# Softmax sums by ones in the values, two of eight copies of distances moved to ScalarE, and probabilities turned two steps after they are made

## The reference

```python
h = _layernorm(x) * (1 + ca) + sa
Q, K, V = h @ Wq + bq, h @ Wk + bk, h @ Wv + bv          # 16 heads of 8
scores = Q @ K.T / sqrt(8) + einsum('bhid,ijd->bhij', Q, rel_table[clip(j - i + 64, 0, 128)])
ctx = softmax(scores) @ V
x = x + ga * (ctx @ Wo + bo)
h = _layernorm(x) * (1 + cb) + sb
x = x + gb * ffn(h)      # a router picks 2 of 8 experts for each token
```

## Time and profile before

| | |
|---|---|
| median of 3 runs | 684.85 us (684.81 to 685.73) |
| profiled execution: time, span | 685.29, 683.6 us |
| busy: PE, PEld | 588.5 us (86%), 439.8 (64%) |
| busy: DVE, ACT, POOL | 507.1 (74%), 508.8 (74%), 423.3 (62%) |
| copies of distances, DVE L1267 | 125 of 0.945 us in the page |
| exps, ACT L711 | 512 of 0.504, and 512 reads of the accumulator of 0.196 |
| turns, PE L968 | 1024 transposes |

### The profile page before, as it was taken

One profiled execution on the slowest core, in us unless ns is written; L12 is line 12 of the kernel. 1 busy time (PEld: TensorE's weight loads), 2 busy tenths in 40 slices (PEclk: granted clock), 3 DMA queues, 4 the chain that ended last, 5 costly groups with the idle time before them and its releaser, 6 DMA issues. The chain is left out here.

```text
span 683.6 us, 17706 instructions
## 1 busy us (share of the span) xinstructions
PE 588.5 (86%) x5108; PEld 439.8 (64%) x5108; DVE 507.1 (74%) x1888; ACT 508.8 (74%) x1578; POOL 423.3 (62%) x543
## 2 busy tenths in 40 slices
PE   5667789999899899899989989978798989999950
PEld 4444556666666566566666656655577979999940
DVE  6788988999999999999999999997565312222127
ACT  4157799999999999999989999998643434444434
POOL 2660655747668687686776966855366765554535
PEclk9777999999999999999999999999999999999975
DMA  5996678778787788778868878874525777565538
GB/s 142 308 230 202 198 235 248 228 235 248 214 245 241 213 252 246 228 219 260 249 208 242 252 213 247 243 236 148 189 82 174 236 234 228 198 217 185 176 97 274
DMA packets 173125, 149.03 MB, mean 218 GB/s; under 512 B 16182, under 2 KB 162642, under 8 KB 173030
## 3 DMA queue, kind: packets, MB, share of 16 engines
q1 hardware_dynamic: 168054, 139.33, 67.9%
q0 software_dynamic: 4544, 8.44, 3.7%
q10 hardware_dynamic: 432, 0.14, 0.1%
HBM read 83.71 MB, written 65.05 MB: 218 GB/s over the span
## 5 line engine op out<-in xcount | busy, mean ns | idle before, releaser
L711 ACT ACTIVATE P<-NS,nmax 128x256 f32<-128x256 f32 x512 | 254.2, 504 | 50.5 <-DVE nmax L1312 49.6
L1312 DVE CUSTOM_DVE_ANT_0 NS<-psS,bias 128x256 f32<-128x256 f32 x512 | 185.2, 417 | 2.3 <-PE psS L950 1.6
L968 PE MATMUL psT<-ident,P 128*128 128x128 f32 x1024 | 140.0, 281 | 8.9 <-ACT PT L722 8.8
L1267 DVE COPY stage<-psDist 128x768 f32<-128x768 f32 x125 | 118.1, 945 | 33.9 <-issue 25.2
L722 ACT ACTIVATE PT<-psT 128x512 f32<-128x512 f32 x256 | 136.4, 586 | 0.0
L968 PEld LDWEIGHTS psT<-ident,P 128*128 128x128 f32 x1024 | 118.2, 145 | 24.0 <-issue 9.8
L778 ACT ACTIVATE F<-psS,b1T 128x256 f32<-128x256 f32 x156 | 65.4, 471 | 86.5 <-PE psS L1061 86.5
L609 POOL DMA_INDIRECT results_d<-y,row_u x78 | 76.0, 974 | 56.7 <-DVE y L1458 40.8
L711 ACT ACTIVATION_READ_ACCUMULATOR P<-NS,nmax 128x1 f32 x512 | 100.3, 196 | 0.0
L950 PE MATMUL psS<-Kst,Qst 32*128 32x256 f32 x512 | 65.9, 336 | 34.7 <-DVE nmax L1312 29.9
L1061 PE MATMUL psS<-xT,w 128*128 128x256 f32 x312 | 80.6, 381 | 0.3 <-DMA w<-in_L_ffn_w_dram 0.3
(11 more groups left out here) (254 smaller groups left out, 1044.2 us busy)
## 6 DMA issues: line engine op xcount, KB each, us to landing
dist_d<-stage SPq DMA_DIRECT2D x128, 384.0 KB, 3.0
bias<-dist_d SPq DMA_DIRECT2D x256, 192.0 KB, 3.3
w<-in_L_ffn_w_dram SPq DMA_DIRECT2D x39, 512.0 KB, 3.7
x<-slots_d SPq DMA_DIRECT2D x39, 129.0 KB, 3.0
y<-results_d SPq DMA_DIRECT2D x16, 256.0 KB, 5.0
dist_d<-zeros SPq DMA_DIRECT2D x1, 2048.0 KB, 14.4
out_dram<-y SPq DMA_DIRECT2D x8, 256.0 KB, 3.2
results_d<-y,row_u POOLq DMA_INDIRECT x78, 3.0
```

The lines of the kernel that those rows point to most:

```text
L711: act.activation(P[:, p % 2, h, q, :], NS[:, p % 2, h, q, :], ACT.Exp, scale=-1.0, bias=nmax[:, p % 2, k:k + 1], accum_out=lsum[:, b % 2, ...
L968: mm = pe.transpose(psT[:, h, S * k + 128 * q:S * k + 128 * q + 128], P[:, p % 2, h, q, 128 * k:128 * k + 128], ident[:])
L1267: dve.tensor_copy(stage[:, p % STAGES, :, :, :], bank[:, :, 0:2 * RW].rearrange("p h (q c) -> p h q c", q=2)).then_inc(dist_out, 1)
L1312: dve.tensor_tensor_reduce(NS[:, p % 2, h, q, :], psS[:, h, S * q:S * q + S], bias[:, p, h, q, :], 1.0, 3e38, ALU.add, ALU.min, nmax[:, p ...
```

## The change

1. *Sums by ones.* The values `V` get a column of ones beside each head's eight columns (16 to a head), two groups of heads share 32 columns, and `psO` is used whole: the row sums come out of `weigh`. The exps lose `accum_out`. `inverses`, `widen`, `spread_l` and `sums` go. ACT copies `psO` to `C` (`copy_values`, p3), PE transposes it, four transposes (`turn_values`, p3), and DVE takes reciprocals and multiplies in `context`, now in p4 behind the minima. The context has tokens on partitions then: PE transposes it (`ct`, p4, in place of `y`), ACT copies it to `ctxT`.
2. *Gains.* `ga` is folded into the weights: for each batch the extra `gain` (p7) spreads two rows over the partitions by matmuls, and DVE makes `boR` and `WoG`. POOL adds the bias to `X` (`add_bias`). The extra `y` (p6) projects with `WoG`; DVE adds it to `X`.
3. *Copies.* In p0 and p4 (`BY_ACT_OUT`) of batches above 0, ACT does the copy of distances, behind its exps and gathers.
4. *Turns.* Probabilities are turned two steps behind (`BEHIND`), with three buffers `P`; `W_SLOTS` follows. ACT's exps stand ahead of the takes.
5. *Loads.* `Wo` and `bv` are permuted on the host: two transfers for eight.

```diff
+BY_ACT_OUT = (0, 4)
 M_SLOTS = ((("q23", 1),), (("k01", 1),), (("k23", 1),), (("logits", -3), ("v", 1)),
-           (("y", -1), ("nh", 2)), (("u01", -2),), (("u23", -2),), (("q01", 2),))
-X_SLOTS = ((), (("rank", -4),), (("turn", -2),), (("back", -2),), (("tally", 1 - B),), (("rows", -3),), (("t", -1),), ())
+           (("ct", -1), ("nh", 2)), (("u01", -2),), (("u23", -2),), (("q01", 2),))
+X_SLOTS = ((), (("rank", -4),), (("turn", -2),), (("back", -2),), (("gains", 0), ("tally", 1 - B)), (("rows", -3),),
+           (("y", -1),), (("gain", 0),))
-W_SLOTS = ((2, (1,)), (3, (0,)), (3, (1,)), None, (0, (0, 1)), (1, (0,)), (1, (1,)), (2, (0,)))
+W_SLOTS = ((2, (0,)), (2, (1,)), (3, (0, 1)), None, (0, (0,)), (0, (1,)), (1, (0,)), (1, (1,)))
+BEHIND = 2
-BY_ACT = ("y", "nh", "back")
+BY_ACT = ("ct", "nh", "back")
...
# SP
-            for a in range(4):
-                at = slice(32 * a, 32 * a + 32)
-                sp.dma_start(WoD[at, :], Wo.rearrange("(g a d) e -> a g d e", a=4, d=D)[a]).then_inc(weights_in, 16)
-                sp.dma_start(bvT[at, :], bv.rearrange("(g a d x) -> a g d x", a=4, d=D, x=1)[a],
-                             allow_slow_non_contiguous=True).then_inc(weights_in, 16)
+            sp.dma_start(WoD[:], Wo).then_inc(weights_in, 16)
+            sp.dma_start(bvT[:], bv.rearrange("(e a) -> e a", a=1)).then_inc(weights_in, 16)
...
# POOL
+            def add_bias(r):
+                at = slice(2 * r, 2 * r + 2)
+                pool.wait_ge(x_dve, X_TAKEN["gain", r][0])
+                pool.tensor_tensor(X[:, at, :], X[:, at, :], rep(boR[:], 1, 2), ALU.add).then_inc(biased, 1)
...
# ACT
-                past(act, turned, 2 * (s - 1))
+                past(act, turned, 2 * (s - BEHIND))
...
-                    act.activation(P[:, p % 2, h, q, :], NS[:, p % 2, h, q, :], ACT.Exp, scale=-1.0,
-                                   bias=nmax[:, p % 2, k:k + 1],
-                                   accum_out=lsum[:, b % 2, q, a, p // 2:p // 2 + 1]).then_inc(exp_done, 1)
+                    act.activation(P[:, s % (BEHIND + 1), h, q, :], NS[:, p % 2, h, q, :], ACT.Exp, scale=-1.0,
+                                   bias=nmax[:, p % 2, k:k + 1]).then_inc(exp_done, 1)
...
+            def copy_values(b):
+                act.wait_ge(values_done, HG * b + HG)
+                past(act, ctx_full, b)
+                act.activation(C[:], psO[:], ACT.Copy).then_inc(c_copied, 1)
+
+            def put_out(n):
+                act.wait_ge(dist_done, n + 1)
+                act.wait_ge(written[(n - STAGES) % SLOTS], 16 * ((n - STAGES) // SLOTS) + 16)
+                act.activation(stage[:, n % STAGES, :, :, :],
+                               psD[:, :, 0:2 * RW].rearrange("p h (q c) -> p h q c", q=2), ACT.Copy)\
+                    .then_inc(dist_out, 1)
...
                 if p == 3 and b > 0:
-                    sums(b - 1)
+                    copy_values(b - 1)
+                exps(b, p)
                 for name, of in M_OF.get(at, ()):
                     if name in BY_ACT:
                         act.wait_ge(m_full, M_DONE[at][0] + 1)
                         take(name, of, psM)
-                exps(b, p)
-                if (b, p) > (0, 0):
-                    gather(*at)
+                if PAIRS * b + p >= BEHIND:
+                    gather(*shifted(b, p, -BEHIND))
+                if act_puts_out(b, p):
+                    past(act, x_dve, so_far(X_DONE, b, p)[1])
+                    past(act, x_act, so_far(X_DONE, b, p)[2])
+                    put_out(PAIRS * b + p + AHEAD)
...
# PE
+                elif name == "gain":
+                    for k in range(2):
+                        mm = pe.matmul(spare[:, k, :], ident[:, r:r + 1].broadcast_to([128, 128]), gR[:, k, :],
+                                       start=True, stop=True)
...
+            def turn_values(b):
+                pe.wait_ge(c_copied, b + 1)
                 for q in range(2):
-                    mm = pe.transpose(psO[:, S + 128 * q:S + 128 * q + 128],
-                                      linvD[:, q, :, :, :].rearrange("p a g d -> p (a g d)"), ident[:])
+                    for r in range(2):
+                        mm = pe.transpose(psO[:, S * q + 128 * r:S * q + 128 * r + 128],
+                                          C[:, S * r + 128 * q:S * r + 128 * q + 128], ident[:])
                 mm.then_inc(ctx_full, 1)
...
# DVE
+                elif name == "gain":
+                    dve.tensor_copy(boR[:], spare[:, 1, :])
+                    i = dve.tensor_tensor(WoG[:], WoD[:], spare[:, 0, :], ALU.mult)
...
             def context(b):
-                dve.wait_ge(lrow_done, b + 1)
+                values = psO[:].rearrange("p (n m d) -> p n m d", n=4, d=2 * D)
+                dve.wait_ge(ctx_full, b + 1)
+                dve.reciprocal(linv[:], values[:, :, :, D:D + 1].rearrange("p n m d -> p n (m d)")).then_inc(linv_done, 1)
                 if b > 0:
-                    dve.wait_ge(m_full, M_FULL["y", b - 1])
-                dve.tensor_tensor(ctxT[:], psO[:, 0:S], lrow[:], ALU.mult).then_inc(ctx_done, 1)
+                    dve.wait_ge(m_full, M_FULL["ct", b - 1])
+                dve.wait_ge(linv_done, b + 1)
+                dve.tensor_tensor(ctx_r[:].rearrange("p q (r m d) -> p (q r) m d", r=2, d=D), values[:, :, :, 0:D],
+                                  rep(linv[:], 3, D), ALU.mult).then_inc(ctx_done, 1)
...
+                if p == 4 and b > 0:
+                    context(b - 1)
...
-                if p == 0 and b > 0:
-                    inverses(b - 1)
...
-                if p == 3 and b > 0:
-                    context(b - 1)
...
-                if n < STEPS:
+                if n < STEPS and not act_puts_out(b, p):
```

More of the change, by code:

```diff
@@ L645, in _ @@
                     stack(b + 1, (b + 1) % 2, 2)
+                if b > 0:
+                    add_bias(b - 1)
                 for r in SENDS.get(b, ()):
@@ L656, in _ @@
                     mix(b - 2, 0)
+            add_bias(B - 1)
             normalise_again(B - 2)
-            widen(B - 1)
             mix(B - 3, 1)
@@ L729, in take @@
                 else:
[L730 to L731 removed]
+                    i = act.activation(ctxT[:], bank[:, 0:S], ACT.Copy)
                 i.then_inc(m_act, 1)
@@ L797, in _ @@
             for b in range(B):
-                if b == 1:
-                    act.wait_ge(taken, 3)
                 for p in range(PAIRS):
                     step(b, p)
-            gather(B - 1, PAIRS - 1)
+            for p in range(PAIRS - BEHIND, PAIRS):
+                gather(B - 1, p)
             act.activation(p1[:, 0:1], ident[:, 0:1], ACT.Silu)
-            sums(B - 1)
-            act.wait_ge(m_full, M_FULL["y", B - 1])
-            take("y", B - 1, banks[1])
+            copy_values(B - 1)
+            act.wait_ge(m_full, M_FULL["ct", B - 1])
+            take("ct", B - 1, banks[1])
             units(0, 1)
@@ L862, in project @@
                                        hT[:, 128 * k:128 * k + 128], Wv_s[:], start=True, stop=True)
-                elif name == "y":
+                elif name == "ct":
                     pe.wait_ge(ctx_done, b + 1)
-                    mm = pe.matmul(bank[:, 0:S], WoD[:], ctxT[:], start=True, stop=True)
+                    for k in range(2):
+                        mm = pe.transpose(bank[:, 128 * k:128 * k + 128], ctx_r[:, k, :], ident[:])
                 elif name in ("u01", "u23"):
@@ L898, in extra @@
                         mm = pe.transpose(spare[:, k, :], h2T[:, 128 * k:128 * k + 128], ident[:])
-                elif name == "t":
-                    pe.wait_ge(m_act, M_TAKEN["y", r][1])
+                elif name == "y":
+                    pe.wait_ge(m_act, M_TAKEN["ct", r][1])
+                    pe.wait_ge(x_dve, X_TAKEN["gain", r][0])
                     for k in range(2):
-                        mm = pe.transpose(spare[:, k, :], yT[:, 128 * k:128 * k + 128], ident[:])
+                        mm = pe.matmul(spare[:, k, :], ctxT[:, 128 * k:128 * k + 128], WoG[:], start=True, stop=True)
+                elif name == "gains":
+                    pe.wait_ge(taken, 3)
+                    pe.transpose(spare[0:B, 0, :], modT[:, 2, :], ident[:])
+                    mm = pe.transpose(spare[0:B, 1, :], gabo[:], ident[:])
+                elif name == "gain":
+                    for k in range(2):
+                        mm = pe.matmul(spare[:, k, :], ident[:, r:r + 1].broadcast_to([128, 128]), gR[:, k, :],
+                                       start=True, stop=True)
                 elif name == "tally":
@@ L1023, in step @@
                     extras()
-                if (b, p) > (0, 0):
-                    turn(*before(b, p))
+                if PAIRS * b + p >= BEHIND:
+                    turn(*shifted(b, p, -BEHIND))
                 if p in X_LATE:
@@ L1033, in step @@
                     weigh(b - int(p < 4), g, halves)
-                    if p == 2:
```

(11 more changed lines are left out.)

80 lines of the change are left out of this document (34 added, 46 removed).

## The result

The changed kernel takes 699.97 us (median of 4; 698.87 to 704.78) beside 685.02 for the kernel before on the same chip: a ratio of 1.0226, 95% interval 1.0194 to 1.0258, slower by about 15. The profiled execution took 699.71, its span is 698.0; before it was 683.6.

A forecast was written before the change was run, and what follows sets the result against it. It took PE and DVE as almost equal in p0 to p5, with PE's work filling the time to p5's scores, and DVE binding from p5. Terms summed to +6.35, giving a 691.2 us median; 8 in 10 range 668 to 697.

The forecast's parts named there:

- Even batches ...: to p5 0, then unchanged, `gain` 0.4: Even batches 4 to 14: nothing lost up to p5, later steps unchanged, `gain` 0.4 each; 6 x 0.4 = 2.4 slower.
- a lighter ACT: All steps: ACT lighter by about 1.6 a batch, booked at nothing because PE and DVE set the steps.
- Odd batches: Odd batches 5 to 13: `gain` 0.4 plus 0.45 for `rank` less 0.1, 5 x 0.75 = 3.75 slower.
- the term for `rank`: p1 of odd batches from 5: PE, and DVE with it, waits 0.45 for ACT's copy ahead of `rank`.
- gain: End of p7: DVE's pair of instructions adds 0.4 a batch with nothing to cover it; ends 0.25 and 0.7.
- Prices: Instruction costs: ACT's copy 0.79 (0.59 to 0.96), exps 0.40 apart, 29 copies on ACT, DVE's p0 step 2.08.
- Turning two steps behind: PE's wait for gathers, 0.3 a batch, goes; 0.1 taken in batches other than even ones; ends 0 and 0.3.
- Batches 1 to 3: First batches after batch 0: 0.3 slower each, 3 x 0.3 = 0.9.
- Start: Before the first minimum: six fewer early issues on SP let distance writes land sooner, 1.3 off; ends 0 and 2.1.
- Last batch and closing: Last batch and end: ACT's saved reads against an added turn, gathers, chain and `add_bias`; 0, ends -2 and +2.
- The faster one: DVE's copies stop waiting for PE; p5's scores under 17.0 after the batch's first minimum; 666 us (655 to 683), chance 0.30.
- No change: ACT's copies come before PE does, and savings in p0 and gathers pay for `gain`; 685 us within 0.2%, chance 0.12.

The follow-up runs named there:

- e8: Changed kernel with two links of the choice moved: `chosen` from p6 to p7, `ahead_of` from p5 to p6; 693.88 us, 1.0109 of the kernel before.
- e13: Changed kernel with both links moved, and ACT's copy of p0 ahead of its gathers in odd batches from 5 on; 690.76 us, 1.0077 of the kernel before.
- e10: Changed kernel with both links moved, DVE's two `gain` instructions cut to a one-column copy in every batch but the first; 686.77 us, 1.0001 of the kernel before.
- e16: Changed kernel with both links moved and probabilities turned one step behind in place of two; 690.57 us, 1.0083 of the kernel before.
- e6: Kernel before, with only the exps' sums into the accumulator left out (a constant 16 instead); 688.30 us, 1.0019 of the kernel before.
- e12: Kernel before with both links moved and `Wo` and `bv` loaded whole in place of eight pieces; 681.61 us, 0.9941 of the kernel before.
- e3: Changed kernel with ACT's copy of distances ahead of the two gathers of its step; 700.10 us, 1.0223 of the kernel before.
- e7: Changed kernel with both links moved, `gain` in next batch's p0, ACT's p0 copy before its gathers, no ACT copy in the last batch; 691.06 us, 1.0080.

## Why the prediction was wrong

**The step that failed** is "Even batches ...: to p5 0, then unchanged, `gain` 0.4", and with it the booking of a lighter ACT at nothing because "PE and DVE set the steps". Up to p5 it held: the scores of p5 begin 17.9 to 18.2 after the batch's first minimum in the even batches, 17.99 in the mean (17.8 forecast). Then p6 was not unchanged. The sum counted what a faster ACT would spare and not what it would set off: the tanh, hence POOL's product, 0.37 earlier, into an instruction of DVE that cleared it by 0.11 before. That is 0.88 in each of six batches, 5.3 of the 8.0 that the sum is short. With both links moved the kernel takes 693.88 (e8), near the forecast 691.2; part of that is luck, since the move also frees `ahead_of`, which was blocked before the change too. The trace of before held the warning: POOL's wait for the tanh says that POOL follows ACT, and of the two groups of `ahead_of`, of one size, one ran 0.89 in the mean and the other 0.42, which the prediction did not use:

```profile
L1347 DVE TENSOR_TENSOR ahead_of<-logit 128x256 f32<-128x256 f32 x6 | 5.4, 892 | 0.6
...
L1350 DVE TENSOR_TENSOR ahead_of<-ahead_of,least 128x256 f32<-128x256 f32 x5 | 2.1, 416 | 0.0
```

**Odd batches** were right in sum, 3.83 for 3.75, and nearly in the term for `rank`: 0.45 forecast, 0.56 by e13. Some of that is luck: p5 is 0.38 a batch longer, and p2 to p4 and p6 together 0.57 shorter.

**gain**: 0.4 forecast at the end of p7, 0.39 measured, and e10 shows that nothing covers it.

**Prices**: ACT's copy 0.80 for 0.79, exps 0.40 apart, 29 copies on ACT, p0's step 2.06 for 2.08, each as said. Turning two steps behind: within what e16 can tell of the 0.1 taken.

**Batches 1 to 3**, 0.9 forecast, 0.03 measured: p7 grew by 1.39, and the other steps together shrank by 1.36. A lighter ACT alone takes 1.31 off these three batches in e6, 1.12 of it in p6; which part of the change paid here wasn't tested.

**Start**: the mechanism right, the size off: 1.3 with ends of 0 and 2.1, measured 2.67, and 2.49 by e12 alone. The fifth copy's wait, which the sum took for the ceiling, was not the only one: in e12 it falls from 2.12 to 0.17, and that of the sixth copy from 0.72 to 0.23, which together is 2.44.

**Last batch and closing**, 0 forecast (-2 to +2), came to 1.80 and 3.04. Windows (granted clock third from the right) of the first 16 us of the last batch, before, after, and with the early copy of e3:

```profile
457.83:473.83 16.00, 12.21 (x113) 8.21 (x112) 11.56 (x55) 14.13 (x49) 8.73 (x14) 0.89 0.63 190
```

```profile
467.39:483.39 16.00, 12.81 (x100) 8.68 (x104) 8.45 (x45) 11.22 (x25) 7.84 (x13) 0.68 0.62 185
```

```profile
465.90:481.90 16.00, 11.82 (x131) 7.62 (x133) 12.37 (x65) 14.49 (x33) 7.93 (x13) 1.00 0.74 216
```

After the change PE stands 1.36 ahead of `rank` for ACT's copy, where it stood 0.58 for DVE's before. The sum had no wait there. e13, with the early copy, has none either, and p1 of its last batch is 0.84 shorter than e8's: that is what the wait costs. The remainder goes with the clock, but not with that wait. PE runs at the 1.2 GHz level for 10 us after the change (0.68 of 16 us) and for 3.5 before (0.89), and the eight transposes of p1 take 1.95 in both, for 1.12 in e3:

```profile
461.63 1.95 PE L968 MATMUL psT<-ident,P 128*128 128x128 f32 x8
```

```profile
472.21 1.95 PE L989 MATMUL psT<-ident,P 128*128 128x128 f32 x8
```

Without the wait for ACT's copy the clock of e13 falls all the same, to 0.68 over these 16 us, and its last batch takes 24.60; e7, where PE stands 1.02 ahead of `rank` for DVE's copy, stays at 1.00 and takes 21.93. Where the clock does not fall at all, the last batch takes 22.33 in the form of the kernel before (e12) and 21.40 after (e3). What sets how long the clock stays low is not shown by these runs; the sum had no term for it.

Of the 3.04 behind it, 0.5 is the closing: from the last step's first minimum to the first up-projection 13.21 before and 13.72 after, with `add_bias` (0.73) ahead of a normalisation on POOL. That this is the reason wasn't tested. Most of the remainder is the FFN, whose code is the same. From its first up-projection to its last it takes 156.5 before and 158.7 after, and the windows show where:

```profile
523.00:528.00 5.00, 4.25 (x30) 4.02 (x31) 2.57 (x15) 1.42 (x4) 2.04 (x3) 1.00 0.19 39
528.00:533.00 5.00, 5.00 (x36) 4.64 (x35) 4.02 (x19) 1.94 (x5) 3.78 (x5) 1.00 0.71 210
```

```profile
535.00:540.00 5.00, 4.39 (x16) 4.06 (x17) 1.72 (x11) 0.84 (x2) 1.94 (x2) 0.51 0.05 16
540.00:545.00 5.00, 5.00 (x31) 4.51 (x30) 2.74 (x11) 1.51 (x4) 3.83 (x4) 0.80 0.60 183
```

The first pair is the kernel before, the second the one after, at the same place of the FFN, behind the same idle time of PE (2.53 and 2.52 ahead of the last `rank`). The clock falls in one and not in the other.

**The rivals.** The faster one was to show scores of p5 before 17.0; they came at 17.99 in the mean, and DVE's wait ahead of its copies did not go. The rule of the Trainium skill that stood behind it (Trainium Kernel Development and Optimization, Performance Expectations), to go by the busy share of weight loads and not by that of matmuls, is given there for the distance from roofline, which no run here measures. Read as a sign of what PE can hide, it did not serve: in batch 8 after the change weight loads are busy 18.80 of 29.82 and matmuls 26.81, and the scores of p5 came no earlier. "No change" had ACT's copies come before PE does; PE waited for them, 0.56 ahead of `rank`.

## What to carry to other kernels

When an engine gets faster, follow what it releases: an earlier start on another engine can meet an instruction that it used to miss, and in the profile such a meeting is no wait but a row that lasts longer than its like. Before a change, compare the mean of each small two-input DVE instruction with one of the same size elsewhere, and note by how much it clears POOL's rows. A profiled execution is one of several: see first whether its time is near the median, and which stretch makes the difference. Where three engines are within 10% of each other, work moved to another step is a gain only if that step has room for it on each engine that it touches: leaving `gain` out of p7 kept the time, and moving it to p0 did not.
